# Pairwise network: two second layers in a row, then two third layers

## The reference

```python
h = jnp.einsum('bsd,fd->bsf', xn, W1)
pair = jax.nn.relu(h[:, :, None, :] - h[:, None, :, :] + b1)
pair = jax.nn.relu(jnp.einsum('bijf,gf->bijg', pair, W2) + b2)
sim = jnp.einsum('bijg,og->bijo', pair, W3)[..., 0] + b3[0]
sim = sim.at[:, diag, diag].set(0.0)
_, top_idx = jax.lax.top_k(sim, k_sparse)
```

## Time and profile before

| | before |
|---|---|
| median of 3 runs | 3087.8 us |
| span of the profiled execution | 3062.4 us |
| the profiled execution's own time | the page gives its span alone; the median lies 25.4 us above it |
| mean granted TensorE clock over the span | 0.940 |
| PE, DVE, ACT, POOL busy | 96%, 60%, 40%, 9% |
| stage of the pairwise network | about 1100 to 2282 us |

### The profile page before, as it was taken

How to read it: one execution, slowest core, us unless ns; L and a number is a source line. 1 busy time by engine, 2 the same in 40 slices (tenths; PEclk the granted TensorE clock), 3 DMA queues, 4 the chain that set the end, 5 groups by cost and what they waited for, 6 DMA issues and landing times. The chain is left out here.

```text
span 3062.4 us, 43851 instructions
## 1 busy us (share of the span) xinstructions
PE 2928.4 (96%) x12449; PEld 1073.4 (35%) x12449; DVE 1843.2 (60%) x4717; ACT 1210.5 (40%) x1398; POOL 284.9 (9%) x579
## 2 busy tenths in 40 slices
PE   7987999999999689999999999999989999999997
PEld 3433555555555322222222222222221222222224
DVE  4553222232222678888888888888875765465554
ACT  4543222222222344544544544555443444343341
POOL 0000000000000211222221222122210000000001
PEclk9998999999999789999999999999996998698787
DMA  1003333333333320000000000000000000000000
GB/s 58 1 5 77 87 92 85 95 86 85 93 84 84 110 41 0 0 0 0 0 0 0 0 0 0 0 0 0 0 14 7 15 15 15 8 15 15 11 4 28
DMA packets 130703, 94.19 MB, mean 31 GB/s; under 512 B 86456, under 2 KB 120760, under 8 KB 130616
## 3 DMA queue, kind: packets, MB, share of 16 engines
q1 hardware_dynamic: 130624, 93.21, 11.2%
HBM read 78.95 MB, written 14.22 MB: 30 GB/s over the span
## 5 line engine op out<-in xcount | busy, mean ns | idle before, releaser
L1261 PE MATMUL spre<-sunit,w2t 128*64 128x512 f32 x4096 | 938.0, 600 | 10.3 <-DVE sunit L1155 10.3
L1155 DVE TENSOR_SCALAR sunit<-hneg,sshift 128x512 f32 x2048 | 842.5, 477 | 27.3 <-POOL sshift L1141 23.3
L1227 ACT ACTIVATE sunit<-spre,b 128x1024 f32<-128x1024 f32 x512 | 570.6, 1114 | 595.7 <-PE spre L1261 595.7
L1261 PEld LDWEIGHTS spre<-sunit,w2t 128*64 128x64 f32 x4096 | 272.0, 137 | 664.9 <-issue 639.4
L1559 DVE CUSTOM_DVE_ANT_0 bjunk<-bs,bmask_s 128x512 bf16<-128x512 f32 x512 | 346.9, 691 | 231.4 <-PE bs L1397 210.5
L1509 ACT ACTIVATE bpt<-bs 128x1024 f32<-128x1024 f32 x256 | 261.9, 1023 | 420.7 <-PE bs L1417 420.7
L801 DVE TENSOR_TENSOR esgs<-egu,esg 128x512 f32<-128x512 f32 x144 | 99.6, 691 | 521.6 <-ACT esg L784 312.0
L761 PE MATMUL egu<-xt,wg 128*128 x576 | 272.6, 596 | 4.5 <-issue 4.5
L1271 PE MATMUL ssims<-sunit,swindow 128*32 128x512 f32 x2048 | 272.8, 605 | 0.0
L761 PE MATMUL egu<-xt,wu 128*128 x576 | 271.9, 594 | 0.0
L741 PE MATMUL eacc<-wd,ehid 128*128 128x256 f32 x1152 | 271.8, 381 | 0.1
(11 more groups left out here) (243 smaller groups left out, 1722.7 us busy)
## 6 DMA issues: line engine op xcount, KB each, us to landing
eshares<-shares SPq DMA_DIRECT2D x144, 256.0 KB, 3.7
wg<-L_ffn_wg SPq DMA_DIRECT2D x128, 64.0 KB, 2.2
wu<-L_ffn_wu SPq DMA_DIRECT2D x128, 64.0 KB, 2.2
wd<-L_ffn_wd SPq DMA_DIRECT2D x64, 128.0 KB, 2.1
q_parts<-pfill SPq DMA_DIRECT2D x4, 1024.0 KB, 8.5
k_parts<-pfill SPq DMA_DIRECT2D x4, 1024.0 KB, 11.8
bqs<-q_parts SPq DMA_DIRECT2D x32, 128.0 KB, 2.3
bks<-k_parts SPq DMA_DIRECT2D x32, 128.0 KB, 2.6
```

What stands on the lines that cost most here:

```text
L1155: ve.tensor_scalar(unit1[:, u, j, :], k.hneg[:, bass.ds(b * S, S)], shift[:, u, j // 2, j % 2:j % 2 + 1], 0.0, ALU.add, ALU.max).then_inc( ...
L1227: act.activation(unit2[:, v, 2 * h:2 * h + 2, :], pre[:, h, :, :], ACT.Relu, bias=b2[:, 0:1]).then_inc(hidden, 1)
L1261: mm = pe.matmul(pre[s * KW:(s + 1) * KW, h, c % 2, :], k.w2t[:, :], unit1[:, u, 2 * c + s, :], start=True, stop=True)
```

## The change

PE's order becomes: second(u), second(u+1), third(u-2), third(u-1), for u = 2, 4, ... 14. At the end of a tile come second(16) and second(17), the first two steps of the next tile, then the mask, third(14) and third(15). The tile is written out on PE without an inner loop. ACT's order follows: it is two steps ahead of the tile's end instead of one, and its inner loop has 4 steps. The ring `unit2` grows from 2 to 4 steps. The third layer reads its 32 columns straight from `bands`, so POOL's copies, the ring `window` and the semaphore `windowed` go. DVE's program is unchanged.

```diff
+    PAIR = 2
-        window = sb("window", [P, R, 32])
-        unit2 = sb("unit2", [P, 2, 4, S])
+        unit2 = sb("unit2", [P, R, 4, S])
...
-                        pool.wait_ge(summed, t + 1)
-                        pause(pool, k)
-                        pool.tensor_copy(window[:, u, :],
-                                         bands[:, bass.ds(m * (32 * R) + 32 * u, 32)]).then_inc(windowed, 1)
...
-                act.wait_ge(summed, t + (AHEAD3 - 1))
+                act.wait_ge(summed, t + (AHEAD3 - R + 1))
...
-            step_done(act, 0, 0)
+            for u in range(PAIR):
+                step_done(act, u, u)
             with act.Fori(0, TILES - 1) as n:
-                with act.Fori(0, STEPS // 2) as m:
-                    for v in range(2):
-                        step_done(act, n * STEPS + m * 2 + (1 + v), 1 - v)
+                with act.Fori(0, STEPS // R) as m:
+                    for v in range(R):
+                        step_done(act, n * STEPS + m * R + (PAIR + v), (PAIR + v) % R)
                 tile_done(act, n)
...
-        def third_layer(pe, n, t, u, first=False):
-            pe.wait_ge(windowed, t + 1)
-            pe.wait_ge(hidden, t * 2 + 2 + AHEAD2)
-            if first:
+        def third_layer(pe, n, t0, u):
+            pe.wait_ge(hidden, t0 * 2 + (2 * u + 2 + AHEAD2))
+            if u == 0:
                 pe.wait_ge(sim_out, n + 1)
             for c in range(4):
-                mm = pe.matmul(simp[32 * c:32 * c + 32, :], window[:, u, :], unit2[:, u % 2, c, :], start=first,
-                               stop=False, skip_group_check=True)
+                mm = pe.matmul(simp[32 * c:32 * c + 32, :], bands[:, 32 * u:32 * u + 32], unit2[:, u % R, c, :],
+                               start=u == 0, stop=False, skip_group_check=True)
             mm.then_inc(summed, 1)
...
         def tile(pe, n, more):
             t0 = n * STEPS
-            for u in range(1, R):
-                second_layer(pe, t0 + u, u)
-                third_layer(pe, n, t0 + u - 1, u - 1, first=u == 1)
-            with pe.Fori(0, STEPS // R - 1) as m:
-                for u in range(R):
-                    t = t0 + m * R + (R + u)
-                    second_layer(pe, t, u)
-                    third_layer(pe, n, t - 1, (u - 1) % R)
+            for u in range(PAIR, STEPS, PAIR):
+                for v in range(u, u + PAIR):
+                    second_layer(pe, t0 + v, v % R)
+                for v in range(u - PAIR, u):
+                    third_layer(pe, n, t0, v)
             if more:
-                second_layer(pe, t0 + STEPS, 0)
+                for v in range(PAIR):
+                    second_layer(pe, t0 + STEPS + v, v)
             turn_mask(pe, n)
-            third_layer(pe, n, t0 + STEPS - 1, R - 1)
+            for v in range(STEPS - PAIR, STEPS):
+                third_layer(pe, n, t0, v)
```

More of the change, by code:

```diff
@@ L1109, in pairwise @@
     AHEAD3 = R
-    shifted, windowed, units, products, hidden, summed, sim_out, search = (k.sem("s_" + n) for n in (
-        "shifted", "windowed", "units", "products", "hidden", "summed", "sim_out", "search"))
+    shifted, units, products, hidden, summed, sim_out, search = (k.sem("s_" + n) for n in (
+        "shifted", "units", "products", "hidden", "summed", "sim_out", "search"))
     mask_made, mask_turned, mask_kept = k.sem("s_mask_made"), k.sem("s_mask_turned"), k.sem("s_mask_kept")
@@ L1240, in _ @@
             act.sem_inc(mask_kept, 1)
-            step_done(act, 0, 0)
+            for u in range(PAIR):
+                step_done(act, u, u)
             with act.Fori(0, TILES - 1) as n:
-                with act.Fori(0, STEPS // 2) as m:
-                    for v in range(2):
-                        step_done(act, n * STEPS + m * 2 + (1 + v), 1 - v)
+                with act.Fori(0, STEPS // R) as m:
+                    for v in range(R):
+                        step_done(act, n * STEPS + m * R + (PAIR + v), (PAIR + v) % R)
                 tile_done(act, n)
             t0 = (TILES - 1) * STEPS
[L1249 to L1252, removed]
+            with act.Fori(0, STEPS // R - 1) as m:
+                for v in range(R):
+                    step_done(act, m * R + (t0 + PAIR + v), (PAIR + v) % R)
+            for u in range(STEPS - R + PAIR, STEPS):
+                step_done(act, t0 + u, u % R)
             tile_done(act, TILES - 1)
@@ L1303, in _ @@
             pe.sem_inc(mask_turned, 1)
-            second_layer(pe, 0, 0)
+            for v in range(PAIR):
+                second_layer(pe, v, v)
             with pe.Fori(0, TILES - 1) as n:
```

## The result

| | before | changed |
|---|---|---|
| median | 3087.7 us (4 runs, 3076.7 to 3096.3) | 3137.1 us (4 runs, 3126.3 to 3174.6) |
| ratio | | 1.0152, 95% interval 1.0108 to 1.0196 |
| profiled execution, its span | 3062.4 us | 3172.9 us |
| time per tile (from one `sim` to the next) | 73.61 us | 78.51 us |
| first second layer to last third layer | 1180.0 us | 1250.6 us |

The kernel became slower by 1.5%; 3148 us had been forecast. The medians are over all executions, and a ratio leaves out those that lie over 1.5% above the fastest of the same kernel, here that of 3174.63 us.

What follows compares the result with a forecast made beforehand. PE was taken to bound the pairwise stage. 15 boundaries x (4.2 us wait + 2.3 us clock) = 97.5, minus 38 saved, gave +60 on 3087.8: 3148 us; own range 3138 to 3158, with rivals A and D 3112 to 3174.

Steps and rivals of the forecast that it cites:

- The saving: PE's changes between second and third layer: 0.30 us less per removed round trip, 8 in each of 16 tiles, 38 us.
- rival C: Gap at PE's changes of layer stays, so nothing is saved: +97 us, 3185 us; chance 7%.
- Weights in place, POOL, ACT, PE's long loop: Reading `bands`, dropped `window` copies, ACT's waits and PE's written-out tile: each 0, with 31 us as bound for the loop.
- Second layer behind second layer: PE's wait for ACT's first half of the step before: 0, at most 0.14 us x 128 = 18 us.
- Rival D: Forecast case with a further PE wait each tile or pair: some +18 us, 3166 us; chance 13%.
- The stall: PE behind third(15) waits for units through ACT and DVE: 4.2 us at each of 15 tile boundaries.
- Rival B: DVE's refill stays off PE's path at the boundaries, only 38 us saved: 3050 us; chance 5%.
- The clock: PE drops to half clock after each boundary wait: 2.3 us lost each time, bounds 0 and 2.95.
- Rival A: PE waits at the boundaries but its clock does not fall: +31 us, 3119 us; chance 20%.
- The sum: Whole kernel: 15 x (4.2 + 2.3) = 97.5 us minus 38, +60 us, giving 3148 us.
- Outside the span: The 25.4 us between profiled span and median of the kernel before run outside the span and stay untouched.
- DVE's wait for `sim`: DVE's wait at tile boundaries for ACT's `sim` falls well below 10.7 us.

Runs made afterwards that it cites:

- pair1: The changed kernel with groups of one layer instead of pairs: 73.61 us a tile, stage 1179.9 us, ratio 0.997 to the kernel before.
- search_later: The changed kernel, but DVE makes the units of steps 2 and 3 ahead of `begin_search`: 71.30 us a tile, ratio 0.985 to the kernel before.
- filler: The changed kernel plus 8 idle PE products behind third(15) of each tile but the last: 76.02 us a tile, ratio 1.010 to the kernel before.
- edge_single: The changed kernel with pairs inside the tile but single layers at its edge, DVE's program kept: 71.73 us a tile, ratio 0.987 to the kernel before.

## Why the prediction was right, step by step

- **What bounds the stage**: PE, with DVE ahead. Right; pair1 and search_later fill it to the last us.
- **The saving**: 0.30 us for each change and back was 0.289, 37.0 us in all (search_later's stage is 37.0 us shorter than before's). Right, and rival C, nothing saved, is out.
- **Weights in place, POOL, ACT, PE's long loop**: counted at 0, and 0.1 us together in pair1; in the changed kernel no instruction fetch falls between 1250 and 2280 us. **Second layer behind second layer**: also counted at 0. The pairs keep 8.87 us in the changed kernel (1981.12 to 1989.99), 8.86 expected, and search_later's 71.30 us a tile has no room for the 18 us. Rival D, a further wait, is out.
- **The stall**: 4.2 us at 15 boundaries were worked out; 4.18 us of idle and 4.24 of delay were measured. Right, as a chain of single instructions. Rival B, no stall, is out: search_later is what it described, and needed another order on DVE.
- **The clock**: the fall was right, 15 of 15; the size was too small. I took 2.3 us; it was 6.0 us at half, a loss of 3.0. My upper bound, from the gap of 4.47 us, was the better row. The lower bound came from 3.4 us at half at 2421.5, but in the ten microseconds before these PE had no idle of 0.2 us or more, so that row was not of this case. Rival A, no fall, is what filler shows. 71.30 + 4.24 + 3.0 = 78.5 us, the tile measured. The Trainium skill's warning in "TensorE: Matmul & The Clock Gate", Why this matters for your kernels, which is against idle gaps of some microseconds between bursts, agrees with the trace at 4.2 us (15 of 15). At 3.6 us the clock fell in 11 of 15, so there the warning held in part.
- **The sum**: +60 us forecast, +70.6 in the stage. The 15 clocks make 10.5 of this difference. The upper end of my own range was added up wrongly by 1 us: 15 x (4.2 + 2.95) - 38 = 69, so 3157 and not 3158. The whole came to +49 because less time lay behind the stage than in the executions of before: taking from the medians the 1.7 us outside the span and what lies ahead of the stage's end in the profiles leaves about 785 us against 804. With 804 the time would have been about 3156, near the upper end of that range. That 3148 came so near to 3137 is partly luck.
- **Outside the span**: wrong. I put the 25.4 us between the span of before and the median down to what runs outside the profile. The changed kernel's execution of 3174.63 us has a span of 3172.9, so only 1.7 us lie outside; the profiled execution of before had less time behind the stage (781 us) than the median leaves (804). No effect on the difference.
- **DVE's wait for `sim`**: wrong. I wrote that it would fall well below 10.7 us. It rose to 17.2, on average by 6.35 us a tile. DVE's work per tile hardly changed (840.6 against 842.5 us of units), so the 4.9 us that a tile grew by come out as more of this wait. So do some 1.4 us a tile that DVE waited ahead of its units before (27.3 us in all, now 5.8), mostly for POOL. PE waits for DVE in turn at another place.

## What to carry to other kernels

An engine with much idle time can still be what the engine that sets the time waits for. Follow its program order, and look at where it gives its surplus back. When work is taken from behind a point where a loop closes (a sum that must be done before the next tile's data can be made), count what the bound engine still has in hand there against the length of the chain; here 4.6 us in hand covered 4.2, and taking it away cost more than eight changes of layer gave. Then try the same grouping with the edge left as it was (edge_single, 1.3% faster here), or with the next data made ahead of the point where the loop closes (search_later, 1.5% faster).

## What the runs showed of the hardware that was not expected

- In all four profiles with the 4.18 us stall the tile time went from 78.32 to 78.45 us at first to 78.51 and stayed there; in the two of the changed kernel the slow stretch went from 5.6 or 5.7 to 6.0 us. So this loop settled to one length. Why at this one, no run shows.
- The same gap of 3.58 or 3.59 us in the same loop left the clock alone in 4 cases and halved it in 11, in four of these only after PE had gone on.
- The same second attention took 770 to 827 us from one execution to another, with a mean granted clock of 0.83 to 0.76.
